# Where the last values product stands among the output projections and the turns of a decoder kernel

## What is computed

```
x = x + self_attention(layernorm(x))            # 16 heads of 32: 6 scaled dot, 4 hyperbolic, 6 cosine; causal
x = x + cross_attention(layernorm(x), context)  # 16 heads, q from x, k and v from the context
x = x + experts(layernorm(x))                   # 8 heads, top 8 of 128x128 experts, gathered rows
```

## Time and profile before

| | us |
|---|---|
| median of 3 runs (lowest, highest) | 2709.6 (2706.38, 2710.87) |
| the profiled execution, its own time | 2701.66 |
| its span, first to last instruction | 2699.9 |
| attention, from the start to the last store | about 1411 |
| experts, from there to the end | about 1289 |
| TensorE busy, DVE busy | 2374.3, 1849.5 |
| mean granted TensorE clock | 0.965 |

### The profile page before, as it was taken

How to read it: one execution, slowest core, us unless ns; L and a number is a source line. 1 busy time by engine, 2 the same in 40 slices (tenths; PEclk the granted TensorE clock), 3 DMA queues, 4 the chain that set the end, 5 groups by cost and what they waited for, 6 DMA issues and landing times. The chain is left out here.

```text
span 2699.9 us, 37982 instructions
## 1 busy us (share of the span) xinstructions
PE 2374.3 (88%) x12584; PEld 1274.5 (47%) x12584; DVE 1849.5 (69%) x5421; ACT 1193.3 (44%) x3236; POOL 1133.8 (42%) x1097
## 2 busy tenths in 40 slices
PE   6899999999999999999767799898988888897776
PEld 3455565555656556565544344344434434343222
DVE  3476765766657576675645897877778687878555
ACT  1457374673736647365443243343334333433322
POOL 2121111212112121111002676777777777777775
PEclk9899999999999999999778899999999999999999
DMA  5000001000010000100002999999999999999998
GB/s 177 8 24 15 24 2 37 1 15 24 2 37 1 15 24 5 34 1 8 1 33 68 370 384 355 403 398 407 385 407 398 395 397 406 400 392 404 404 411 349
DMA packets 158050, 514.38 MB, mean 191 GB/s; under 512 B 16960, under 2 KB 27200, under 8 KB 157856
## 3 DMA queue, kind: packets, MB, share of 16 engines
q0 software_dynamic: 129024, 469.82, 44.3%
q1 hardware_dynamic: 27248, 40.62, 4.5%
q10 hardware_dynamic: 1584, 1.52, 0.2%
HBM read 504.56 MB, written 7.34 MB: 190 GB/s over the span
## 5 line engine op out<-in xcount | busy, mean ns | idle before, releaser
L1519 POOL DMA_INDIRECT e_rows<-in_experts,e_idx x896 | 894.1, 998 | 343.7 <-issue 287.7
L1573 PE MATMUL e_ps_out<-e_rows,e_diag 128*128 128x512 f32 x1792 | 836.7, 612 | 151.6 <-ACT e_diag L1848 151.4
L1737 DVE CUSTOM_DVE_ANT_0 e_rows<-e_rows,xn_all 128x512 f32<-128x512 f32 x896 | 567.0, 688 | 242.1 <-DMA e_rows<-in_experts,e_idx 241.5
L1573 PEld LDWEIGHTS e_ps_out<-e_rows,e_diag 128*128 128x128 f32 x1792 | 339.4, 195 | 599.8 <-issue 431.1
L1848 ACT ACTIVATE e_diag<-ident_f,e_weight 128x128 f32<-128x128 f32 x896 | 286.2, 390 | 306.7 <-DVE e_weight L1748 300.4
L915 DVE SCALAR_TENSOR_TENSOR ring<-ps_s,mask 112x750 f32<-112x750 f32 x256 | 232.7, 935 | 149.4 <-PE ps_s L525 113.8
L1099 ACT ACTIVATE ring<-ring,neg_max 112x750 f32<-112x750 f32 x256 | 233.4, 913 | 164.0 <-DVE neg_max L925 164.0
L536 PE MATMUL ps_t<-ident,ring 112*125 112x112 f32 x1536 | 232.9, 290 | 46.5 <-ACT prob_t L1112 37.1
L536 PEld LDWEIGHTS ps_t<-ident,ring 112*125 112x125 f32 x1536 | 198.1, 195 | 123.5 <-ACT ring L1099 59.1
L1843 ACT ACTIVATE e_active<-e_hidden 128x4 f32<-128x4 f32 x224 | 46.0, 205 | 467.7 <-DVE e_hidden L1737 467.4
L1112 ACT COPY prob_t<-ps_t 125x336 f32<-125x336 f32 x512 | 200.0, 440 | 98.6 <-PE ps_t L536 98.2
(11 more groups left out here) (184 smaller groups left out, 2882.8 us busy)
## 6 DMA issues: line engine op xcount, KB each, us to landing
e_rows<-in_experts,e_idx POOLq DMA_INDIRECT x896, 6.7
ctx_t<-in_ctx_t SPq DMA_DIRECT2D x8, 1500.0 KB, 6.5
e_w_q<-in_ffn_wq SPq DMA_DIRECT2D x16, 256.0 KB, 7.0
x_in<-in_x SPq DMA_DIRECT2D x8, 448.0 KB, 3.6
x_dram<-x SPq DMA_DIRECT2D x8, 448.0 KB, 3.1
acc<-x_dram SPq DMA_DIRECT2D x7, 512.0 KB, 6.8
out<-acc SPq DMA_DIRECT2D x14, 256.0 KB, 6.0
w_qkv<-in_w_qkv_t SPq DMA_DIRECT2D x3, 1024.0 KB, 10.3
```

The costliest lines, as they stand in the source:

```text
L1519: pool.indirect_dma_start(rows[:, v % RING, k, :], None, table[:, :], bass.IndirectOffsetOnAxis(ap=idx[:, e:e + 1], axis=0))\
L1573: mm = nc.tensor.matmul(ps_out[t % 2][:], diag[:, HU * (v % ND) + k, :], rows[:, v % RING, k, D:], start=(s == 0 and k == 0), stop=(s == S ...
L1737: last = nc.vector.tensor_tensor_reduce(down, down, xn_all[:, t, :], 1.0, 0.0, ALU.mult, ALU.add, hidden[:, b, k:k + 1])
```

## The change

Two of the four quarters of values group 5 are issued between the spread of the inverse sums and the projections, one between the turned tile 0 and the turned tile 1, and one stays where it was, behind tile 1. The sum over the quarters is made in the same order in the same bank, and no semaphore is added or dropped; the group's wait for `ps_y` (`v_ready` of group 4) is now met ahead of the projections.

```diff
                 pe.wait_ge(k_ready.sem, k_ready.at(b, 2 * KC))
                 spread_sums(b, 0)
+                values_group(b, NC - 1, prev, range(KC - 2))
                 for t in range(NT):
                     pe.wait_ge(act_ready.sem, act_ready.at(b, t + 1))
                     for kc in range(KC):
                         project(bank[t], w_proj, t, kc)
-                values_group(b, NC - 1, prev, range(KC - 1))
                 for t in range(NT):
+                    if t == 1:
+                        values_group(b, NC - 1, prev, range(KC - 2, KC - 1))
                     pe.wait_ge(xn_ready.sem, xn_ready.at(b, NT + t + 1))
                     for c in range(KC):
                         mm = nc.tensor.transpose(ps_t[t][:, c * TT:(c + 1) * TT], x_n[:, t, c * P:(c + 1) * P],
```

## The result

The changed kernel takes 2741.2 us (median of 4 runs, 2739.6 to 2742.8) against 2709.7 before (2706.4 to 2710.9). The ratio is 1.012 with a 95% interval of 1.0104 to 1.0135: 31.5 us slower, where the forecast was 21.7. The profiled execution took 2739.55 us, with a span of 2737.8.

What follows compares the result with a forecast made beforehand. In the attention tail, TensorE and DVE hand on one chain that sets the queries' start. Order +15.4 us and clock +6.3 us sum to 21.7 over the median 2709.6, so 2731 us; range 2719 to 2742.

Steps and rivals of the forecast that it cites:

- falls behind the projections: Low clock after the new pause, stretching the queries: six falls in the other seven batches at 1.41 us, +8.5 us.
- Step 1: Two quarters ahead of the projections: 1.72 us on TensorE, 0.08 hidden, so projections come 1.64 us later per batch.
- Step 2: Three quarters taken from behind the projections: gain 0, since the turns wait for x_n; 2.68 us become idle.
- Step 3: One quarter between the turns: tile 1's transposes 0.32 us late per batch, hidden in the eighth.
- Step 4: Last quarter, values_out, the copies and the 1.84 us wait before the queries stay as they are: 0.
- Order in all: Order costs of the tails summed: 1.96 us in seven batches and 1.64 in the eighth, 15.4 us.
- falls at the projections: Low clock as the spread ends, 10.95 us over five batches: one fall of five taken as gone, -2.2 us.
- (b): Rival: low clock throughout the tail, queries starting at 1.2 GHz in every batch: +36 us, 2746; chance 0.12.
- (a): Rival: order only, the clock gives back as much as it takes: +15.4 us, 2725; chance 0.22.
- (c): Rival: full-row work right behind the spread ends the projections' falls and queries keep their clock: +3.0 us, 2713; chance 0.06.
- (d): Rival: a later stage, such as cross-attention, absorbs the delay, so the 1.96 us vanish: 2710; chance 0.05.

Runs made afterwards that it cites:

- before_emptied: Kernel before with three of the four quarters of values group 5 left out, so the pause behind the projections is empty: 2721.3 us, ratio 1.0051.
- quarter_between: Kernel before with only one quarter moved between the turned tiles, two left behind the projections, none ahead of them: 2703.9 us, ratio 0.999.
- copies_first: Kernel before with DVE's two copies of the turned tiles put ahead of values_out: 2687.5 us, ratio 0.9923.
- changed_filled: Changed kernel with six records of idle matmuls in the pause between the projections and the first turn: 2723.1 us, ratio 1.0061 to before.
- half_ahead: Kernel before with two quarters moved ahead of the projections, the third kept behind them, the fourth behind the turns: 2748.7 us, ratio 1.0152.
- half_ahead_longer: half_ahead with two quarters of values group 2 made twice, far from the tail: 2916.7 us beside 2871.0 for before, ratio 1.0155.
- half_ahead_of_spread: half_ahead with its two early quarters put ahead of the last weigh step of self-attention, so ahead of the spread: 2718.7 us, ratio 1.0042 to before.
- copies_first_quarter_early: copies_first with one quarter ahead of self-attention's last weigh step, two behind the projections, one behind the turns: 2684.5 us, ratio 0.9915 to before.
- quarter_early: Kernel before with one quarter moved ahead of self-attention's last weigh step, DVE's order unchanged: 2868.9 us beside 2871.0, ratio 0.9989.

## Why the prediction was right and wrong

The direction held, and so did the order part of the sum and the cause named for the rest, a pause that costs clock. The size didn't: 31.5 us slower where 21.7 were forecast, at the very end of the range (2741.2 against 2742; the ratio of 1.012 on 2709.6 gives 2742.1). The step that failed is the price of the falls behind the projections. By its steps:

- Step 1, 1.64 us a batch: the first turn is 1.73 later behind the spread (13.32 against 11.59). The first projection is 1.82 later, at my upper bound of 1.8. The cover that I counted at 0.08 was not there.
- Step 2, nothing saved and 2.68 us idle: 2.51 shown as idle, ended by DVE x_n. Right; before_emptied shows that the quarters had been hidden entirely.
- Step 3, 0.32: 0.26, measured alone in quarter_between, and nothing in the eighth batch. Right.
- Step 4, nothing: the wait of 1.84 stands. Right, and it was the best place in the tail to look for a gain: copies_first.
- Order in all: 15.4 forecast, 15.7 in the tails. changed_filled, which keeps the order and fills the pause, is 16.2 over before; that this is so near is in part luck, as its trace has 5.1 us less lost at the spread than before's and 3.7 more behind the first turn.
- The falls at the projections, -2.2: -3.3. Right in size, but by luck: half_ahead and half_ahead_longer show that the same order in the tail can have seven such falls or one. What I summed up before, 10.95, is 11.8 by the starts, as two of the falls began within the spread.
- The falls behind the projections, +8.5: +14.9. This is the step that failed. "Six falls in all seven" was right as a count: of the seven batches all but the third lost. But I priced a fall at 1.41 us, the loss of the queries alone in the eighth batch, and put a loss in the turns and quarters at nothing, and the eighth batch too. The six falls cost 13.2 us, 1.5 to 3.4 each, and the eighth 1.8 more than before. 9.3 of the 14.9 us were lost ahead of the queries, where the low clock doubles quarters that now stand in the chain (0.86 to 1.74 at the fifth batch); the queries themselves lost 5.6, less than the 8.5 forecast, and began at the low clock in four batches of eight, not in most. My upper bound of 21 for the whole covered it; its 2.97 a batch did not cover the fifth and the sixth (3.4). Why a fall comes early in one batch and late in another isn't shown.

One reading of the range doesn't come out: half-way from 2731 to the 2746 of rival (b) is 2738.7, not 2742.

With the measured terms the sum is 15.7 - 3.3 + 14.9 = 27.3 us. The 4.2 us between this, which is from one profile of each kernel, and the medians' 31.5 aren't placed; they are within what executions of one kernel differ by: the first spread starts at 118.1 us in before_emptied and at 122.4 in quarter_between, whose code up to there is the same. What made the experts' part 5.6 us longer in the one profile isn't shown.

Of the rivals, (a), order only, is excluded: the pause has its price in both directions, 15 to 18 us in changed_filled and 14 in before_emptied. (b) was half right: the queries begin low in four batches, but recover. (c) is half refuted. Full-width work right behind the spread doesn't prevent the fall there (half_ahead: seven of eight). Where it stands ahead of the last weigh step there are few falls (half_ahead_of_spread: one of eight; copies_first_quarter_early and quarter_early: none), but half_ahead_longer and quarter_between have only one and two without it, so that its place is what does it is likely and not shown. (d) is excluded by the constant 141.25 us between tails: nothing later takes up the delay.

The Trainium skill's rule that activity releases the low clock ("TensorE: Matmul & The Clock Gate", Part 1, section "What's actually happening") agrees with changed_filled, where 48 records of useless work save 15 to 18 us. Its Part 4 says of transposes that they don't count as busy in the same way; by it I gave all seven new falls; six came. The runs leave this rule open: quarter_between turns the same tiles and keeps its queries at 6.32 in seven tails, changed_filled in five, while its other three fall though the pause is filled.

## What to carry to other kernels

In this kernel work that filled another engine's latency was free twice: it was hidden, and it helped to keep TensorE's clock. Moving it ahead of the chain was paid for twice, as work on the chain (15.7 us) and as slower matmuls behind the pause that it left (14.9 us). When you price a fall of the clock, count everything on the chain that it can stretch, not only the group where you saw it. Read such a tail for what stands in the queue ahead of the instruction that is waited for: here an order of three lines on DVE was worth 20 us, 16 of them by the order itself, with nothing moved on TensorE.

## What was unexpected of the hardware

- Falls of the clock can repeat from batch to batch, and go with an edit far away. half_ahead's profile has the fall at the spread in seven of eight tails, most of them 170.8 to 171.1 us apart; with 1.7 us of idle work per batch, at nearly the same distances, it is in one of eight and the tails are 10 us shorter. So a difference of 10 us between two such kernels need not come from the edit's own place.
- Leaving out three quarters of a matmul group made the kernel 14.4 us slower (before_emptied), and adding 48 records made it 15 to 18 us faster (changed_filled against changed).
- A shorter pause was not a cheaper one: 1.65 us in half_ahead came with 28.6 us lost behind the first turn, 2.51 us in the changed kernel with 16.4.
